# The last batch of a fused cross-attention kernel: products five and six change places, and the first row's root and one scaling are placed earlier

## The reference

```python
memory_proj = einsum('bme,de->bmd', memory, W_mem)
scores = einsum('bnd,bmd->bnm', hidden_states, memory_proj) / sqrt(D)
attn = softmax(scores)
memory_context = einsum('bnm,bmd->bnd', attn, memory_proj)
gate = sigmoid(einsum('bnf,df->bnd', concat([hidden_states, memory_context]), W_gate) + b_gate)
fused = hidden_states + gate * memory_context
return fused * rsqrt(mean(fused ** 2) + EPS) * norm_w
```

## Time and profile before

| what | value |
|---|---|
| median of 3 runs | 919.98 us (919.16 to 5234.18) |
| the profiled execution's own time | 920.19 us |
| its span, first to last instruction | 918.5 us |
| PE busy, share of the span | 907.8 us, 99% |
| PE weight loads | 765.2 us, 83% |
| DVE busy | 750.7 us, 82% |
| ACT busy | 424.3 us, 46% |
| POOL busy | 54.3 us, 6% |
| mean granted TensorE clock | 0.998 of full speed |

### The profile page before, as it was taken

How to read it: one execution, slowest core, us unless ns; L and a number is a source line. 1 busy time by engine, 2 the same in 40 slices (tenths; PEclk the granted TensorE clock), 3 DMA queues, 4 the chain that set the end, 5 groups by cost and what they waited for, 6 DMA issues and landing times.

```text
span 918.5 us, 11744 instructions
## 1 busy us (share of the span) xinstructions
PE 907.8 (99%) x4376; PEld 765.2 (83%) x4376; DVE 750.7 (82%) x962; ACT 424.3 (46%) x632; POOL 54.3 (6%) x73
## 2 busy tenths in 40 slices
PE   9999999999999999999999999999999999999996
PEld 7788888888888888888888888888888888888885
DVE  5998666767767989798796589888888988898887
ACT  5542222322232454454646355555555565555553
POOL 0000000000000000000000011110111111111002
PEclk9999999999999999999999999999999999999999
DMA  9314255566544664876879935455655554444542
GB/s 323 111 59 170 93 183 207 186 227 209 204 161 128 255 235 141 294 274 237 295 232 391 373 120 175 173 203 207 207 206 183 194 165 179 172 172 176 207 183 91
DMA packets 56504, 183.74 MB, mean 200 GB/s; under 512 B 5632, under 2 KB 13568, under 8 KB 50944
## 3 DMA queue, kind: packets, MB, share of 16 engines
q1 hardware_dynamic: 56160, 182.47, 56.1%
q10 hardware_dynamic: 288, 0.52, 0.2%
HBM read 127.93 MB, written 55.05 MB: 199 GB/s over the span
## 4 chain that ended last, share of the span: by engine, by line
PE 98%; DVE 1%; DMA 0%; ACT 0%; POOL 0%; issue 0%; DVEq 0%
PE psum L1585 32%; PE psum L1586 32%; PE psum L1587 32%; PE psum L1687 1%; DMA b_came<-in_g 0%; PE psum L1603 0%; PE psum L1607 0%; PE psum L1611 0%; ACT zb L935 0%; DVE xlast L1578 0%; DVE zb L1502 0%; ACT zb L930 0%; POOL stat L666 0%; POOL stat L662 0%; DVE xlast L1508 0%
## 5 line engine op out<-in xcount | busy, mean ns | idle before, releaser
L1585 PE MATMUL psum<-g1h,xh 128*128 128x512 f32 x416 | 161.9, 389 | 0.6 <-issue 0.6
L1586 PE MATMUL psum<-g_l,xh 128*128 128x512 f32 x416 | 161.8, 389 | 0.0
L1585 PEld LDWEIGHTS psum<-g1h,xh 128*128 128x128 f32 x416 | 78.1, 188 | 17.4 <-DVE g_l L987 1.0
L1586 PEld LDWEIGHTS psum<-g_l,xh 128*128 128x128 f32 x416 | 78.1, 188 | 16.0
L1460 DVE TENSOR_TENSOR zb<-psum,zb 128x512 f32<-128x512 f32 x112 | 76.7, 685 | 15.7 <-PE psum L1587 15.7
L1587 PE MATMUL psum<-g1h,xs_l 128*128 128x512 f32 x192 | 74.7, 389 | 0.0
L673 ACT ACTIVATE xh<-xs_raw 128x512 fp32r<-128x512 f32 x48 | 30.3, 632 | 95.7 <-PE psum L1587 95.7
L648 POOL TENSOR_TENSOR stat<-stat 128x1 f32<-128x1 f32 x30 | 19.7, 658 | 845.5 <-ACT zb L923 845.5
L1585 PE MATMUL psum<-yh,ws_h 128*128 128x512 f32 x160 | 62.5, 390 | 0.0
L1587 PE MATMUL psum<-yh,ws_l 128*128 128x512 f32 x160 | 62.3, 389 | 0.0
L1179 DVE TENSOR_TENSOR z<-psum,bias 128x512 f32<-128x512 f32 x48 | 33.1, 691 | 29.9 <-PE psum L1587 29.9
(11 more groups left out here) (200 smaller groups left out, 2512.5 us busy)
## 6 DMA issues: line engine op xcount, KB each, us to landing
b_raw<-in_xt SPq DMA_DIRECT2D x32, 512.0 KB, 8.0
zb<-z_spill SPq DMA_DIRECT2D x16, 1024.0 KB, 6.8
xrow<-in_x SPq DMA_DIRECT2D x30, 512.0 KB, 6.6
out<-xrow SPq DMA_DIRECT2D x30, 512.0 KB, 3.9
xs_raw<-in_xt SPq DMA_DIRECT2D x12, 1024.0 KB, 4.9
z_spill<-z SPq DMA_DIRECT2D x12, 1024.0 KB, 8.4
y_spill<-y SPq DMA_DIRECT2D x40, 256.0 KB, 3.8
yt_raw<-y_spill SPq DMA_DIRECT2D x16, 512.0 KB, 3.8
```

The lines of the kernel that those rows point to most:

```text
L1585: nc.tensor.matmul(tile, ah, mh, start=start, stop=False, skip_group_check=True)
L1586: nc.tensor.matmul(tile, ah, ml, start=False, stop=False, skip_group_check=True)
```

## The change

In the last batch PE runs product 5 ahead of product 4 (`LAST_ORDER`), and the quarters are taken as (0,0), (0,1), (1,1), (1,0) in place of (0,0), (1,1), (0,1), (1,0). `made(b, i)` gives the count at which product i is done in the new order. DVE's z_out and mem_add follow that order. The quarters 0 and 1 are now both of row half 0, so its root needs no later quarter: POOL sums it and takes its power behind the second square. Quarter 1 gets a multiplication with `norm` on DVE directly behind its addition of x, and its scaling goes from DVE to ACT, between the squares of quarters 2 and 3. DVE keeps the scalings of quarters 0 and 2. The diff, cut to its core:

```diff
-        f_norm = mem[:, 1, 0:BANK]
+        f_norm = {1: mem[:, 0, 0:BANK], 3: mem[:, 1, 0:BANK]}
...
-        QUARTERS = [(0, 0), (1, 1), (0, 1), (1, 0)]
+        QUARTERS = [(0, 0), (0, 1), (1, 1), (1, 0)]
+        LAST_ORDER = (0, 1, 2, 3, 5, 4, 6)
+        def made(b, i):
+            return P7 * b + (LAST_ORDER.index(i) if b == B - 1 else i) + 1
...
-            for n, q in enumerate((0, 2, 1)):
+            for q in (1, 0, 2):
                 nb, h = QUARTERS[q]
-                sp.wait_ge(row_done, 2 * (B - 1) + n + 1)
+                if q == 1:
+                    sp.wait_ge(q_scaled, 1)
+                else:
+                    sp.wait_ge(row_done, 2 * (B - 1) + (1 if q == 0 else 2))
...
+            pool.wait_ge(sq_q, 1)
+            pool.tensor_tensor(guarded[:, 0:1], part[:, 0:1], eps, ALU.add).then_inc(guarded_done, 1)
             pool.wait_ge(sq_q, 2)
-            for nb in range(NB):
-                pool.tensor_tensor(guarded[:, nb:nb + 1], part[:, nb:nb + 1], eps, ALU.add).then_inc(guarded_done, 1)
+            pool.wait_ge(guarded_done, 2 * B - 1)
+            pool.tensor_tensor(guarded[:, 0:1], part[:, 1:2], guarded[:, 0:1], ALU.add).then_inc(guarded_done, 1)
+            pool.wait_ge(guarded_done, 2 * B)
+            pool.tensor_tensor(rstd[:, 0:1], guarded[:, 0:1], minus_half, ALU.pow).then_inc(rstd_done, 1)
             pool.wait_ge(sq_q, 3)
-            pool.wait_ge(guarded_done, 2 * B)
-            pool.tensor_tensor(guarded[:, 0:1], part[:, 2:3], guarded[:, 0:1], ALU.add).then_inc(guarded_done, 1)
-            for nb in range(NB):
-                pool.wait_ge(guarded_done, 2 * B + 1 + nb)
-                pool.tensor_tensor(rstd[:, nb:nb + 1], guarded[:, nb:nb + 1], minus_half, ALU.pow
-                                   ).then_inc(rstd_done, 1)
+            pool.tensor_tensor(guarded[:, 1:2], part[:, 2:3], eps, ALU.add).then_inc(guarded_done, 1)
+            pool.wait_ge(guarded_done, 2 * B + 2)
+            pool.tensor_tensor(rstd[:, 1:2], guarded[:, 1:2], minus_half, ALU.pow).then_inc(rstd_done, 1)
...
-                act.wait_ge(z_done, P7 * (B - 1) + (2, 5, 6, 7)[q])
+                act.wait_ge(z_done, made(B - 1, (1, 5, 4, 6)[q]))
...
+            def scale_quarter(q):
+                nb, h = QUARTERS[q]
+                act.wait_ge(fn_done, {1: 1, 3: 2}[q])
+                act.wait_ge(rstd_done, 2 * (B - 1) + nb + 1)
+                nc.scalar.activation(xlast[:, nb, HALF[h]], f_norm[q], ACT.Copy, scale=rstd[:, nb:nb + 1]
+                                     ).then_inc(q_scaled, 1)
...
                     square_quarter(2)
+                    scale_quarter(1)
                     square_quarter(3)
+                    scale_quarter(3)
                     nb, h = QUARTERS[3]
-                    act.wait_ge(fn_done, 1)
-                    act.wait_ge(rstd_done, 2 * B)
-                    nc.scalar.activation(xlast[:, nb, HALF[h]], f_norm, ACT.Copy, scale=rstd[:, nb:nb + 1]
-                                         ).then_inc(q_scaled, 1)
-                    act.wait_ge(q_scaled, 1)
+                    act.wait_ge(q_scaled, 2)
...
-                dve.wait_ge(mem_mm, P7 * b + i + 1)
+                dve.wait_ge(mem_mm, made(b, i))
...
-                dve.wait_ge(gate_mm, P7 * b + i + 1)
+                dve.wait_ge(gate_mm, made(b, i))
...
-                    dve.wait_ge(mem_copied, 4 * b + (1, 3, 2)[q])
+                    dve.wait_ge(mem_copied, 4 * b + (1, 2, 3)[q])
...
-                if q == 3:
+                if q in (1, 3):
                     dve.wait_ge(f_q, q + 1)
-                    nc.vector.tensor_tensor(f_norm, row, norm[:, HALF[h]], ALU.mult).then_inc(fn_done, 1)
+                    nc.vector.tensor_tensor(f_norm[q], row, norm[:, HALF[h]], ALU.mult).then_inc(fn_done, 1)
...
                     fuse_quarter(0)
-                    z_out(b, 4)
-                    mem_add(b, 4)
+                    z_out(b, 5)
+                    mem_add(b, 5)
...
                     fuse_quarter(1)
-                    z_out(b, 5)
-                    mem_add(b, 5)
+                    z_out(b, 4)
+                    mem_add(b, 4)
...
-            for q in (0, 2, 1):
+            for q in (0, 2):
...
-                    if m == 0:
+                    if b == B - 1 and i in (4, 5):
+                        if m == 0:
+                            pe.wait_ge(mem_copied, 4 * b + {5: 3, 4: 2}[i])
+                        else:
+                            pe.wait_ge(z_done, made(b, {5: 3, 4: 2}[i]))
...
-                            pe.wait_ge(mem_added, 3 * b + {3: 1, 6: 2}[i])
+                            pe.wait_ge(mem_added, 3 * b + {3: 1, 6: 3 if b == B - 1 else 2}[i])
...
-                            pe.wait_ge(z_done, P7 * b + {2: 1, 3: 2, 4: 3, 5: 4, 6: 5}[i])
+                            pe.wait_ge(z_done, P7 * b + {2: 1, 3: 2, 4: 3, 5: 4, 6: 6 if b == B - 1 else 5}[i])
...
-                mem_gate(b, 4)
+                mem_gate(b, LAST_ORDER[4] if b == B - 1 else 4)
                 if b + 1 < B:
                     turn_probs(b + 1)
-                mem_gate(b, 5)
+                mem_gate(b, LAST_ORDER[5] if b == B - 1 else 5)
```

More of the change, by code:

```diff
@@ L1760, in mem_gate @@
                             pe.wait_ge(y_copied, 8 * SB)
-                    if m == 0:
+                    if b == B - 1 and i in (4, 5):
[3 more added lines that the diff above has]
+                            pe.wait_ge(z_done, made(b, {5: 3, 4: 2}[i]))
+                    elif m == 0:
                         if i == 0 and b >= 1:
```

## The result

The changed kernel takes 921.54 us (median of 11 runs, 920.13 to 924.42), the kernel before beside it 919.30 us (median of 11, of which ten lie between 918.45 and 920.84 and one took 5234.18). The ratio is 1.0023, with a 95% interval of 1.0014 to 1.0031: a loss of 1.3 to 2.9 us. The forecast was 921.8 us, within 920.4 to 923.3, with no change of 2% or more. It held, and so did nearly all of its steps. One number, the time of the last power on POOL, was right for a reason that was wrong, and the 2.29 us that reach the tail came out exactly because two small errors cancel.

A forecast was written before the change was run, and what follows sets the result against it. PE was taken to set the pace (98% of the chain). Delay of 2.29 us less 0.43 gained in the tail adds 1.86 to the 918.5 span: 920.4, or 921.8 us as median; range 920.4 to 923.3.

The forecast's parts named there:

- the time of the last power on POOL: Row root's final power, behind DVE's small addition in the tail: taken as 1.01 us, since POOL will have paused.
- First pause: PE ahead of product 5's gate group: waits for product 3's z_out, which still reads that bank; 1.17 us.
- the rival value of 921.3: PE's weight loads lie inside both waits, each restart 0.23 us cheaper, the sum below 0.46 less; no chance given.
- Second pause: PE ahead of product 6's gate group: waits for product 4's z_out; 1.34 us, 0.61 to 0.73 from the new multiplication.
- What reaches the tail: PE ends 2.51 us later; DVE's earlier slack leaves product 6's z_out, and the chain behind it, 2.29 later.
- The slack as an argument: Before, PE's last gate group ended at 908.87 but busy DVE began its z_out at 909.13, so some delay is absorbed.
- ACT's early scaling: ACT's 0.72 us scaling of quarter 1 between two squares: fits by 0.1 us, otherwise costs up to its 0.72.
- The tail: From DVE's small addition to the last store issue: one power and one scaling, 2.06 us in place of 2.49.
- The bounds of 0.54 and 1.54: POOL's last power: 0.54 us right behind another, 1.54 behind a long pause; 0.47 off or 0.53 on.
- The last stores: Rival at the end: only two stores issued last, landing in 2.1 us, end 0.7 earlier, 921.1; chance 0.12.
- The clock: Rival: PE's clock falls after the pauses, product 6's twelve matmuls put on 2.4 us, 924.2; chance 0.05.
- Not slower: Rival: PE's stalls do not reach the tail, only DVE's work counts, +0.3 or -0.2 us; chance 0.07.

The follow-up runs named there:

- dve_scales_q1: The changed kernel without quarter 1's early multiplication with norm and ACT's scaling of it; DVE scales quarters 0, 1 and 2 at the end; 921.39 us, ratio 1.0019.
- one_more_wait: The kernel before the change, with one more wait: in the last batch product 4's gate group waits for z_out of product 3; 921.17 us, ratio 1.0012.
- zout_ahead: The changed kernel with DVE's z_out of product 4 ahead of quarter 1's steps, its norm multiplication behind mem_add, ACT's third tanh ahead of the second square; 920.72 us.
- late_s0: The changed kernel with one more small DVE addition, and a wait on it, between the small addition and quarter 0's scaling; 921.75 us, ratio 1.0022.
- all_together: The changed kernel with product 5's context group first, DVE's last-batch steps reordered, quarter 0 scaled by ACT and quarter 1 by DVE at the end; 919.40 us, ratio 0.9999.

## Why the prediction was right

- **First pause, 1.17 forecast, 1.14 measured.** The mechanism is the one named: the weight load of product 5 waits until z_out of product 3 is done (902.74 + 0.69 = 903.43) and starts at 903.54. It did not go ahead of the wait, so the rival value of 921.3 falls. The page of the Trainium skill that the prediction names there (Perfetto Trace Analysis, Tensor Engine Instruction) has weight loads pulled ahead of matmuls in flight; it does not say that a load passes a wait. The restart is put together otherwise than I had it: 0.11 from z_out's end to the load where I took 0.05, a matmul 0.04 behind the load where I took 0.23, and then 0.30 to the second matmul in place of 0.23. In effect PE's stream resumes 906.17 - 2.50 - 903.43 = 0.24 behind the z_out (2.50 being eleven matmuls), where the forecast had 0.28.
- **Second pause, 1.34 forecast, 1.30 measured.** The row ahead of z_out of product 4 is as written: quarter 1's two steps, the multiplication at 908.88, z_out at 909.49. The multiplication's share of 0.61 to 0.73 was 0.71 in dve_scales_q1.
- **What reaches the tail, 2.29 forecast, 2.29 measured** for z_out of product 6, and again for the small addition (915.64 - 902.31 = 13.33, against 11.04). That it fits to the hundredth is luck: the two pauses are 2.44 and not 2.51, and z_out of product 6 starts 0.11 behind the end of PE's last gate matmul (911.55 + 0.39 = 911.94, then 912.05), where the forecast took 0.04. The one error of 0.07 makes up for the other. The slack as an argument held in this kernel, and fails in one_more_wait. It was right here by the place of the pause and not in general.
- **ACT's early scaling** fits, with 0.18 idle ahead of the last square, where 0.1 was forecast.
- **The tail, 2.06 forecast, 2.07 measured**, with a power of 0.99 for 1.01. This is the step whose reason was wrong. The bounds of 0.54 and 1.54 are not a short and a long pause of POOL, as the prediction had them; they tell whether DVE executes an instruction with two SBUF inputs at that time (below). The value came out because in both kernels such an instruction starts shortly ahead of the power, and that is luck. The trace of the kernel before could have shown it. Its power of 1.54 at 871.46 and its power of 1.01 at 912.06 each follow an addition on POOL by less than 0.1 us, so no pause stood ahead of either:

```profile
870.26 1.12 POOL L648 TENSOR_TENSOR stat<-stat 128x1 f32<-128x1 f32 x1 [20.92 <-ACT zb L923]
```

```profile
911.25 0.72 POOL L662 TENSOR_TENSOR stat<-stat 128x1 f32<-128x1 f32 x1 [3.02 <-ACT zb L935]
```

And in the changed kernel an addition behind 3.90 us of idle time took 0.19, with a power of 0.55 right behind it (909.67 and 909.94 above).
- **The last stores.** The rival in which the last one lands in 2.1 falls: the one on ACT's queue took 2.7, near the 2.8 of before, though the three on SP's queue now took 2.0 to 2.3. The page's row on it (KB each, us from issue to landing):

```profile
out<-xlast ACTq DMA_DIRECT2D x1, 256.0 KB, 2.7
```

- **The clock** stays at 1.00, the level of 2.4 GHz, behind both pauses (1.14 and 1.30 us), and that rival falls too.
- **Not slower** falls: both pauses are there and reach the end.
- **The scale.** The profiled execution lies 1.1 above the median of its own runs, and its t0 alone is 0.63 later than before's; the forecast of 921.8 was made from a profile that lay 0.2 above the median shown, and took no such scatter into its steps, only into its range.

## What to carry to other kernels

When two products change places in a stream without pauses, ask for each which bank it adds to and whether that bank's last reader is through. Here the new neighbour of product 3 was a product that adds to the bank which product 3's read-out still reads, and a gain of 0.43 in the tail was bought with 2.29 ahead of it. A pause removed alone may only make the next one longer: read the row of the engine that is waited for to its end, and change the order there together with the stream's. An instruction moved off the tail is free only where its new engine row has a gap; here a multiplication came to stand at the one place of DVE's row for whose end PE was waiting.

## What the runs showed of the hardware

**POOL's small instructions are held back by DVE.** Alone, POOL's addition of 128x1 takes 0.19 and its power 0.55 (909.67 and 909.94 above; DVE was in a z_out and a mem_add then, which read PSUM). If DVE is executing an instruction whose two inputs both lie in SBUF, they end a fixed time after that instruction: the addition 0.05, the power 0.40. Six of the places that show it:

| POOL's instruction | DVE's instruction beside it ends | POOL's ends |
|---|---|---|
| changed, power at 915.88 | 915.72 + 0.74 = 916.46 | 916.87, +0.41 |
| changed, addition at 914.17 | 914.16 + 0.69 = 914.85 | 914.90, +0.05 |
| before, power at 912.06 | 911.97 + 0.69 = 912.66 | 913.07, +0.41 |
| before, power at 871.46 | 871.37 + 1.23 = 872.60 | 873.00, +0.40 |
| zout_ahead, addition at 909.68 | 909.36 + 0.68 = 910.04 | 910.09, +0.05 |
| zout_ahead, power at 910.17 | 909.96 + 0.69 = 910.65 | 911.05, +0.40 |

DVE's row for the earlier batch of the kernel before, and POOL's two of zout_ahead:

```profile
871.37 1.23 DVE L1474 SCALAR_TENSOR_TENSOR xrow<-zb,xrow 128x1024 f32<-128x1024 f32 x1
```

```profile
909.68 0.41 POOL L671 TENSOR_TENSOR stat<-stat 128x1 f32<-128x1 f32 x1 [5.02 <-ACT zb L946]
910.17 0.88 POOL L673 TENSOR_TENSOR stat<-stat 128x1 f32<-128x1 f32 x1
```

The rule holds throughout. From 560 us on, the timelines of the ten traces show 602 additions and powers of 128x1 on POOL each on a line of its own. Of these, 298 had a DVE instruction with two SBUF inputs of 128x512 or more under way at their start, or begun within 0.01 us of it; the additions among them ended 0.04 to 0.06 behind it, the powers 0.40 to 0.42. The other 304 took 0.19 or 0.55.

In dve_scales_q1 three such scalings stand back to back on DVE, and POOL is held for the first only (the first ends at 914.36 + 0.75 = 915.11, the power at 914.52 + 0.99 = 915.51, 0.40 later). Before, a power at 913.04 started 0.06 ahead of a scaling of DVE and took 0.54, and that scaling was not slower than the others either (747, 748 and 752 ns for the three). In late_s0 and all_together the power starts 0.15 ahead of the scaling and takes 0.55. A start only 0.01 ahead is not enough: all_together's power at 911.57 stood beside a step of DVE from 911.58 to 912.26 and ended at 912.67, again 0.41 behind. Where between 0.01 and 0.06 the border lies, no run shows.

By the Trainium skill (SBUF — State Buffer, SBUF: two separate sides) DVE and GpSimd share one port pair under an exclusive lock, held for the whole instruction by whichever starts first, and a DVE instruction with two SBUF inputs takes part against a GpSimd instruction that reads SBUF. The traces agree where DVE's instruction comes first, with +0.05 and +0.40 as its price here, but a hold ends with the first of several such instructions in a row. That the other way round DVE is blocked by POOL does not show in the scaling at 913.10 (0.75 as the others). The prediction had missed this rule and put the same numbers down to pauses.
